# Flamingo-style layer pair: the second cross-attention's keys and queries stacked in half precision, scaled by the context's largest magnitude

## The reference, cut to what matters

```python
x = x + tanh(g_xattn[0]) * cross_attention_0(layernorm(x), ctx, mask)    # first stage
x = x + tanh(g_ffn[0])   * ffn_0(layernorm(x), w_up, w_down)             # ternary weights
x = x + tanh(g_xattn[1]) * cross_attention_1(layernorm(x), ctx)          # the stage of the change
x = x + tanh(g_ffn[1])   * ffn_1(layernorm(x), weight1, weight2, weight3)

def cross_attention_1(qkv, y):          # qkv (4, 512, 512), y (4, 1601, 512)
    bs, width, length = qkv.shape
    ch = width // 16                     # 16 heads of 32 channels
    q = qkv.reshape(bs * 16, ch, length)
    k = v = y.reshape(bs * 16, ch, -1)   # the context's memory read as (channels, 1601)
    scale = 1.0 / sqrt(sqrt(ch))
    weight = softmax(einsum('bct,bcs->bts', q * scale, k * scale))
    return einsum('bts,bcs->bct', weight, v).reshape(bs, -1, length)
```

## Time and profile before

| | |
|---|---|
| median of 3 runs | 1842.4 us (1840.54 to 1844.35) |
| the profiled execution: time, span | 1841.3 us, 1839.5 us |
| TensorE matmuls busy | 1658.9 us (90%), 7540 |
| TensorE weight loads busy | 800.2 us (44%), beside the matmuls |
| VectorE, ScalarE, GpSimd busy | 1147.0, 760.9, 843.0 us |
| mean granted clock of TensorE | 0.959 of 2.4 GHz |

### The profile page before, as it was taken

How to read it: one execution, slowest core, us unless ns; L and a number is a source line. 1 busy time by engine, 2 the same in 40 slices (tenths; PEclk the granted TensorE clock), 3 DMA queues, 4 the chain that set the end, 5 groups by cost and what they waited for, 6 DMA issues and landing times. The chain is left out here.

```text
span 1839.5 us, 22129 instructions
## 1 busy us (share of the span) xinstructions
PE 1658.9 (90%) x7540; PEld 800.2 (44%) x7568; DVE 1147.0 (62%) x1529; ACT 760.9 (41%) x1241; POOL 843.0 (46%) x340
## 2 busy tenths in 40 slices
PE   5999999898777876899999999899999997799898
PEld 2454444444433333444444444444444432344443
DVE  3669989884455557676766676667676630444543
ACT  1321211211543431566666666566666665111110
POOL 0022234544221125577778888677777877000000
PEclk9999999899899995999999999999999999799999
DMA  8232223322111115444333334444433310400000
GB/s 320 80 120 77 83 93 96 103 100 79 39 30 35 34 41 137 113 114 112 77 96 89 98 97 113 114 113 113 113 88 90 77 46 1 95 23 0 23 23 23
DMA packets 134316, 152.57 MB, mean 83 GB/s; under 512 B 59694, under 2 KB 101826, under 8 KB 134214
## 3 DMA queue, kind: packets, MB, share of 16 engines
q1 hardware_dynamic: 129222, 140.76, 29.3%
q10 hardware_dynamic: 4992, 10.49, 1.7%
HBM read 73.42 MB, written 10.76 MB: 46 GB/s over the span
## 5 line engine op out<-in xcount | busy, mean ns | idle before, releaser
L1352 DVE TENSOR_REDUCE c_piece_max<-c_unit 128x1 f32<-128x804 f32 x512 | 485.0, 984 | 241.0 <-PE c_unit L1490 238.4
L1448 ACT ACTIVATE c_prob<-c_scores 128x512 f32<-128x512 f32 (+1 forms) x832 | 473.3, 596 | 267.3 <-PE c_scores L1507 250.5
L1287 POOL TENSOR_TENSOR c_prob_sum<-c_prob_sum,c_prob 128x2048 f32<-128x2048 f32 x96 | 439.4, 4577 | 12.0 <-ACT c_prob L1448 6.0
L1507 PE MATMUL c_scores<-c_queries,c_keys 98*128 98x512 f32 (+1 forms) x832 | 354.8, 443 | 32.7 <-ACT c_prob L1448 17.4
L1490 PE MATMUL c_unit<-c_khigh,c_qdiag 128*128 128x402 f32 x1024 | 303.2, 381 | 20.1 <-DMA c_qdiag<-c_qhigh 10.1
L1490 PEld LDWEIGHTS c_unit<-c_khigh,c_qdiag 128*128 128x128 f32 x1024 | 186.6, 198 | 150.1 <-DVE c_piece_max L1352 90.1
L1507 PEld LDWEIGHTS c_scores<-c_queries,c_keys 98*128 98x128 f32 (+1 forms) x832 | 152.4, 186 | 202.0 <-ACT c_prob L1448 141.3
L1516 PE MATMUL c_out<-c_prob,c_VT 128*32 128x512 f32 (+1 forms) x1664 | 220.8, 610 | 0.0
L641 PE MATMUL a_S<-a_ctxT,a_xnT 128*128 128x401 f32 x512 | 190.7, 517 | 7.2 <-ACT a_prob L598 3.9
L671 PE MATMUL a_o<-a_ctx,a_probT 128*128 128x512 f32 (+1 forms) x416 | 181.2, 592 | 0.0
L1287 POOL TENSOR_TENSOR c_prob_sum<-c_prob 128x2048 f32<-128x2048 f32 x16 | 73.5, 4592 | 121.1 <-ACT c_prob L1448 121.1
(11 more groups left out here) (196 smaller groups left out, 1975.0 us busy)
## 6 DMA issues: line engine op xcount, KB each, us to landing
c_keys<-c_khigh SPq DMA_DIRECT2D x128, 200.2 KB, 3.0
c_k<-in_keys SPq DMA_DIRECT2D x16, 801.0 KB, 6.3
c_keys<-c_k SPq DMA_DIRECT2D x64, 200.2 KB, 3.0
a_ctx<-in_ctx SPq DMA_DIRECT2D x12, 1024.0 KB, 6.8
c_VT<-in_values SPq DMA_DIRECT2D x16, 768.0 KB
a_ctxT<-in_ctxT SPq DMA_DIRECT2D x12, 802.0 KB, 4.7
c_queries<-c_qhigh SPq DMA_DIRECT2D x128, 64.0 KB, 2.6
a_weights<-in_L_ffn_weight SPq DMA_DIRECT2D x3, 1408.0 KB, 14.7
```

The source lines that it names most:

```text
L1287: nc.gpsimd.tensor_tensor(psum4[:], a[:], prob[(j * MC + c) % RING][:], ALU.add).then_inc(sums_taken, 2 if i == 1 else 1)
L1352: nc.vector.tensor_reduce(piece_max[j % 2][:, k // 2, k % 2:k % 2 + 1], U[bank(unit)][:, :, 0:PIECE], axis=AX.XY, op=ALU.max).then_inc(uni ...
L1448: nc.scalar.activation(prob[(j * MC + c) % RING][0:w, h, :], STp[h % 2][0:w, :], ACT.Exp, scale=SCALE).then_inc(exp_done, 1)
L1507: nc.tensor.matmul(STp[h % 2][0:w, :], K[p][:, h, c * P:c * P + w].bitcast(F32R), Q[p][:, h, :].bitcast(F32R), start=True, stop=True).then ...
```

## The change

Half precision (float16) takes the place of float32r in the rounded parts, the rests, the stacks `K` and `Q`, and the block diagonal. Float16 has less range, so the keys are scaled by 2^13 over the largest magnitude of the whole context, and the exponential's scale takes the factor back. For that the first stage reduces each batch's transposed context on VectorE (`context_top`, in steps 2, 6, 10 and 14), joins the four, sends 128 numbers through memory and back to all partitions (SyncE, two DMAs, ahead of the stores of the weights), and makes two factors (`context_scales`). The keys' rest, with the scale in one operation, goes to VectorE, into a buffer of its own; it stands behind the maximum of unit 6 of group g+2. The negative maxima are one half-precision row (times 1/512 against 512 in the keys' row) rather than two: ScalarE's rounding of them and GpSimd's rest go, the row's matmul waits for VectorE's join alone. The waits are renamed to match.

```diff
+KEY_RANGE = 2.0 ** 13
+KEY_SCALE = float(D // 16) ** -0.5
...
             def load_transposed(b):
+                if b > 0:
+                    sp.wait_ge(ctx_topped, b)
...
+            sp.wait_ge(ctx_topped, B + 1)
+            sp.dma_start(flat_ctx_top.rearrange("(p o) -> p o", o=1), ctx_tops[:, B:B + 1]).then_inc(ctx_top_out, 16)
+            sp.wait_ge(ctx_top_out, 16)
+            sp.wait_ge(bit_scales_ready, 1)
+            sp.dma_start(wtops_all[:, 0:P // 4, :].rearrange("p r k -> p (r k)"), flat_ctx_top.rearrange("(o r) -> o r", o=1).broadcast_to([P, P])).then_inc(ctx_top_loaded, 16)
...
+            def context_top(b):
+                for n in range(4):
+                    dve.wait_ge(ctxT_loaded[n], 16 * (b + 1))
+                nc.vector.tensor_reduce(ctx_tops[:, b:b + 1], CT[:], axis=AX.XY, op=ALU.max, apply_absolute_value=True).then_inc(ctx_topped, 1)
+                if b == B - 1:
+                    dve.wait_ge(ctx_topped, B)
+                    nc.vector.tensor_reduce(ctx_tops[:, B:B + 1], ctx_tops[:, 0:B], axis=AX.X, op=ALU.max).then_inc(ctx_topped, 1)
+
+            def context_scales():
+                steps, scales = Steps(dve, ctx_scale_steps), shared["ctx_scales"]
+                dve.wait_ge(ctx_top_loaded, 16)
+                steps.link(nc.vector.tensor_reduce(scales[:, 2:3], wtops_all[:, 0:P // 4, :].rearrange("p r k -> p (r k)"), axis=AX.X, op=ALU.max))
+                steps.link(nc.vector.tensor_scalar(scales[:, 3:4], scales[:, 2:3], 1e-30, 1.0 / KEY_RANGE, ALU.max, ALU.mult))
+                steps.did(nc.vector.reciprocal(scales[:, 0:1], scales[:, 3:4]))
+                steps.did(nc.vector.tensor_scalar(scales[:, 1:2], scales[:, 3:4], KEY_SCALE, None, ALU.mult))
+                steps.settle()
...
+                if k % ST == 2:
+                    context_top(k // ST)
...
             add_out(K - 2)
+            context_scales()
...
-        KA = KM + 2
+        KA = KM + 1
+        ONES = 2.0 ** 9
...
-        krest = [k[:].bitcast(F32R) for k in kt]
-        khigh = [sb(f"c_khigh{j}", [P, MK], F32R) for j in range(2)]
+        krest = [sb(f"c_krest{j}", [P, MK], F16) for j in range(2)]
+        khigh = [sb(f"c_khigh{j}", [P, MK], F16) for j in range(2)]
...
-        K = [sb(f"c_keys{j}", [KA, H, MK]) for j in range(2)]
-        Q = [sb(f"c_queries{j}", [KA, H, D]) for j in range(2)]
+        K = [sb(f"c_keys{j}", [KA, H, MK], F16) for j in range(2)]
+        Q = [sb(f"c_queries{j}", [KA, H, D], F16) for j in range(2)]
...
-                    sp.wait_ge(rests_ready, 2 * n + 2)
+                    sp.wait_ge(qrest_ready, n + 1)
+                    sp.wait_ge(krest_ready, n + 1)
...
-            def rest_of_k(n, j):
-                pool.wait_ge(khigh_ready, n + 1)
-                nc.gpsimd.tensor_tensor(krest[j], kt[j][:], khigh[j][:], ALU.subtract).then_inc(rests_ready, 1)
-
-            def rest_of_maxima(n):
-                pool.wait_ge(nhigh_ready, n + 1)
-                high, rest = [nparts[:, :, :, a].rearrange("p t h -> p h t") for a in range(2)]
-                nc.gpsimd.tensor_tensor(rest, nmax[:], high, ALU.subtract).then_inc(nparts_ready, 1)
...
+            def rest_of_k(n, j):
+                dve.wait_ge(khigh_ready, n + 1)
+                wait(dve, stacked, (n - 1) * STACKS)
+                nc.vector.scalar_tensor_tensor(krest[j][:], kt[j][:], key_scale, khigh[j][:], ALU.mult, ALU.subtract).then_inc(krest_ready, 1)
...
-                nc.vector.tensor_copy(nrow[:], U[bank(unit)][0:2 * H, 0, :]).then_inc(unit_read, 1)
+                nc.vector.tensor_scalar(nrow[:], U[bank(unit)][0:H, 0, :], 1.0 / ONES, None, ALU.mult).then_inc(unit_read, 1)
...
             statistics(0)
             statistics(1)
+            rest_of_k(0, 0)
...
+                    if main and more and unit[2:] == (j + 2, 6):
+                        rest_of_k(g + 2, j % 2)
                 if not main:
+                    rest_of_k(1, 1)
                     statistics(2)
...
-                nc.scalar.copy(khigh[j][:], kt[j][:]).then_inc(khigh_ready, 1)
+                nc.scalar.activation(khigh[j][:], kt[j][:], ACT.Copy, scale=key_scale).then_inc(khigh_ready, 1)
...
-            def high_of_maxima(n):
-                act.wait_ge(nmax_ready, n + 1)
...
             def rows(unit):
                 n = unit[1]
-                pe.wait_ge(nparts_ready, n + 1)
+                pe.wait_ge(nmax_ready, n + 1)
```

More of the change, by code:

```diff
@@ L127, in cross_attention_0 @@
         wtops_all = sb("a_wtops_all", [P, P, 4])
+        ctx_tops = sb("a_ctx_tops", [P, B + 1])
         BIT_PIECES = 4
@@ L1044, in cross_attention_1 @@
     X, ident, gates = shared["X"], shared["ident"], shared["gates"]
+    key_scale, score_scale = shared["ctx_scales"][:, 0:1], shared["ctx_scales"][:, 1:2]
     with ExitStack() as stack:
@@ L1417, in split_queries @@
                 x = X[:, bass.ds(n, 1), :].rearrange("p o d -> p (o d)")
-                wait(act, rests_ready, 2 * n - 1)
+                wait(act, qrest_ready, n)
                 nc.scalar.activation(xn[:], x, ACT.Identity, bias=nshift[:], scale=rstd[:]).then_inc(xn_ready, 1)
@@ L1424, in split_queries @@
                 nc.scalar.copy(qhigh[j][:], xn[:]).then_inc(qhigh_ready, 1)
-            def high_of_maxima(n):
-                act.wait_ge(nmax_ready, n + 1)
-                wait(act, unit_full, FULL0 + rows_place(n - 1) + 1 if not isinstance(n, int) or n > 0 else 0)
-                nc.scalar.copy(nparts[:].bitcast(F32R)[:, :, :, 0].rearrange("p t h -> p h t"), nmax[:]).then_inc(nhigh_ready, 1)
             def take_out(g):
@@ L1465, in slot @@
                         split_keys(g + 2, j % 2)
-                    if c == (8 if not isinstance(g, int) or g > 0 else 10) and nxt:
-                        high_of_maxima(g + 1)
                 if nxt:
@@ L1489, in pair @@
                     at = STARTS[2 * half + e]
-                    last = nc.tensor.matmul(U[bank(unit)][:, e, 0:PIECE], QZ[o][:, h, t * P:(t + 1) * P].bitcast(F32R), khigh[o][:, at:at + PIECE], start=True, stop=True)
+                    last = nc.tensor.matmul(U[bank(unit)][:, e, 0:PIECE], QZ[o][:, h, t * P:(t + 1) * P], khigh[o][:, at:at + PIECE], start=True, stop=True)
                 last.then_inc(unit_full, 1)
@@ L1494, in rows @@
                 n = unit[1]
-                pe.wait_ge(nparts_ready, n + 1)
+                pe.wait_ge(nmax_ready, n + 1)
                 pe.wait_ge(unit_read, rows_place(n) + 1)
                 for t in range(TB):
-                    last = nc.tensor.transpose(U[bank(unit)][0:2 * H, 0, t * P:(t + 1) * P], nparts[:, t, :, :].rearrange("p h a -> p (h a)"), ident[:])
+                    last = nc.tensor.transpose(U[bank(unit)][0:H, 0, t * P:(t + 1) * P], nmax[:, t, :], ident[:])
                 last.then_inc(unit_full, 1)
@@ L1815, in program @@
         weight_tops, bit_scales = weight_stats[:, 0:2], weight_stats[:, 2:4]
+        ctx_scales = stack.enter_context(nc.sbuf_tensor("ctx_scales", [P, 4], F32))
         gates = stack.enter_context(nc.sbuf_tensor("gates", [P, 4], F32))
```

51 lines of the change are left out of this document (23 added, 28 removed).

## The result

The changed kernel takes 1874.6 us in the median of 4 runs (1872.4 to 1878.4), the kernel before 1841.9 beside it: ratio 1.018, 95% interval 1.016 to 1.020. The profiled execution took 1873.7 us with a span of 1871.9. The forecast's sum was 1874.4, slower with a chance of 0.59. The total is right; of its terms several are not, and they cancel.

A forecast was written before the change was run, and what follows sets the result against it. Bound: a chain of exponential, score and output product in second cross-attention, not TensorE's busy time. 1841.3 + 8.4 (first stage) - 5.8 (prologue) + 3 (group 0) + 34 (groups 1-13) - 6.5 (groups 14, 15) = 1874.4 us; range 1806 to 1888.

The forecast's parts named there:

- The half-precision matmuls: Second cross-attention: shorter bare and hidden weight loads save 0.26 us a chunk, 3.1 us a group, 50.4 to 47.3.
- The stall and its clock: Second cross-attention: VectorE's rest waits for GpSimd's addition; chain stops 3.5 us, slow clock adds 2.2, 5.7 a group.
- Other parts 0: Outside the main terms: the stack's DMAs and SyncE's added waits, put at 0; the exponential's scale operand goes unmentioned.
- Groups 1 to 13: Second cross-attention: each group 53.0 us with the stall, 2.6 more than before, +34 us together.
- Granted clock under 0.95 in the slices of this stage: Sign for the second cross-attention: TensorE's granted clock falls below 0.95, with an idle of 3 to 4 us a group.
- Group 0: Second cross-attention's first group: 16 more units, VectorE nearly full and also given the rest, +3 us (0 to 6).
- groups 14 and 15: Second cross-attention's last groups: no keys' rest to make, so no stall, -3.2 us each, -6.5 together.
- The prologue: Second cross-attention's prologue: single row of maxima -2.6 us, shorter loads in 32 units -3.2, together -5.8 (-9 to -2).
- The first stage: Four context reductions of 6.85 us on VectorE: the second and third delay step 12's chain, +8.4 us (5 to 12).
- their chain had some 8 us to spare: First stage's end: the fourth reduction delays the last weights by 6.85 us, held to be covered by this slack.
- Rival 1: Keys' rest meets no addition, or the addition does not hold it: it costs 1 us a group, 1809; chance 0.31.
- Rival 2: Rest is blocked, but the clock stays at 2.4 GHz: 50.8 us a group, 1845 in total; chance 0.11.

The follow-up runs named there:

- e5: Changed kernel with unscaled keys (nothing measured or scaled), a number as the exponential's scale, keys' rest back on GpSimd behind the last addition: 1787.4 us, ratio 0.970.
- e2: Changed kernel with the exponential's scale as a number of this data, the measured scale left out there: 1875.9 us, ratio 1.018.
- e6: Changed kernel with keys' rest behind unit 11, a number as the exponential's scale, no context reductions (finding of the scale left out): 1793.0 us, ratio 0.973.
- e9: Changed kernel with the keys' rest behind unit 11 in place of unit 6, nothing else altered: 1828.4 us, ratio 0.993.
- e3: Changed kernel without the four context reductions, their DMAs and waits, both scales set to this data's numbers: 1856.7 us, ratio 1.008.
- e7: Changed kernel with its context reductions at other places of VectorE's order, their DMAs behind the weights' stores, nothing left out: 1862.5 us, ratio 1.010.
- e10: Changed kernel with the keys' rest in two halves of 801 columns, behind units 6 and 11: 1855.0 us, ratio 1.008.

## Why the prediction was right

Its mechanism was the one that the runs show: the rest on VectorE meets GpSimd's addition of probabilities, is held until it ends, TensorE stops behind it once a group, and the clock falls. Term by term:

- **The half-precision matmuls**, forecast -3.1 us a group. e5 measures -2.5 (50.4 to 47.9). The longest score is 404 ns for 503, as forecast for a bare load; the term is too large by 0.6, and how the 2.5 divides is not shown.
- **The stall and its clock**, forecast 3.5 + 2.2 = 5.7 for a request 0.7 us late. In e2, which is the kernel that the forecast had in mind (an exponential of 595 ns), the request was 0.71 us late, TensorE idle 3.79 us, and the group 53.7 against e6's 48.1: 5.6 us (5.3 by the means of 13 groups). In the changed kernel itself the request came 1.6 us late, the idle time was 2.58, and the price 3.7.
- **The exponential** is the term that the forecast did not have. "Other parts 0" took in that its scale became one value per partition; that costs 88 ns in each, and 1.2 us a group (e9 against e6). It also moved the request by 0.9 us and so made the stall cheaper, which is why leaving it out (e2) changed nothing: -1.2 and +1.9. The forecast's group of 53.0 was right because its errors are of one size: 2.0 too much for the stall against 0.6 too much for the matmuls, 1.2 for the exponential and 0.2 for the moved rest. Most of this is linked, as the exponential made the stall cheaper; that it comes out even is luck. The Trainium skill (ScalarE: Activation LUTs, "What ACT_TABLE_LOAD costs") gives about 93 ns for each operand of one value per partition; these runs have 88.
- **The sum of a group**: 50.4 - 2.5 (e5) + 0.2 (rest on VectorE, e6) + 1.2 (exponential, e9) + 3.7 (lock and clock) = 53.0.
- **Groups 1 to 13**, forecast +34, measured +24.8 (50.9 to 52.8 in the mean). The forecast took 2.6 us for each of the 13. But before, group 8 took 55.9, 5.5 more than its neighbours; after, its extra is 1.8. And in three groups the stall cost no clock, which saves 1.9 each.
- **The clock.** "Granted clock under 0.95 in the slices of this stage" was wrong, it was 0.97. After the stall TensorE mostly ran at 1.2 GHz for a few us, but not always: in 10 of 13 groups. These are two windows around the end of a stall of 2.36 us, in the group of 51.1 us, and of one of 2.58, in a group of 53:

```profile
955.00:962.00 7.00, 6.14 (x45) 1.95 (x45) 4.98 (x6) 3.13 (x5) 6.16 (x4) 1.00 0.01 1
1060.00:1067.00 7.00, 6.59 (x33) 1.92 (x37) 4.01 (x6) 2.69 (x5) 5.79 (x3) 0.77 0.02 3
```

  The difference, 1.9 us, is what the clock costs where it falls (2.2 forecast); the idle time itself costs 51.1 - 49.3 = 1.8, less than its 2.4 to 2.6 us, since part of it was a wait before too.
- **Group 0**, forecast +3, and **groups 14 and 15**, forecast -3.2 each. From the first score to the first sum it takes 60.7 us against 61.7, so -1.0. Groups 14 and 15 gained 1.2 and 0.1 us; with a fast exponential (e2) 2.7 and 3.7. Here the missing term shows bare. The prediction also read 48.5 us for such a group out of a window of 97; between the sums' matmuls it was 47.8 before.
- **The prologue**, forecast -5.8. From TensorE's stop to the first score it was 52.9 us and is 47.2: -5.7. The sign "the first scores at 732" left out the forecast's own +8.4; with it the forecast would be 740.6, and they came at 748.2.
- **The first stage**, forecast +8.4, measured +15.9 up to TensorE's stop ahead of the prologue. Step 12 moved by 10.0 us (331.90 to 341.87), the forecast's chain. The step that failed is "their chain had some 8 us to spare" of the last weights. They were 16.3 us late (the sixth of the weights before them was 9.4 late already, by what had moved step 12, and the fourth reduction added 6.8), and the 8 us belonged to VectorE's own wait for TensorE; the chain that counts goes from the weights to GpSimd's clips, to the store in ScalarE's queue, to the copies behind it.

In all, the 15 groups behind the first sum gave +23.4 (forecast +27.5) and everything ahead of it +9.1 (forecast +5.6). The first stage's 7.5 us too few, and 5.1 too few for groups 14 and 15, stand against 9.2 too many for groups 1 to 13 and 4.0 for group 0. That the total is met within 1 us is luck; that the kernel is slower, and why, is not.

Rival 1 (the request comes before the addition, 1809) did not happen, but a few units later it does: in e9 the rest comes after the last addition, in e6 it meets only its last microsecond, and e6 lies 0.2 us a group above e5, less than the 1 us of that rival. Rival 2 (blocked, but the clock stays) is what 3 of 13 groups did.

## What to carry to other kernels

When work moves from GpSimd to VectorE and both read tensors in SBUF, ask what GpSimd runs at that moment: what VectorE loses is the time until it ends, on top of its own work, and a place of a few units earlier or later makes the difference (53.0 to 49.3 us a group by one number). Then ask who waits for the result: a place too late (unit 14) held SyncE's queue of 24 copies and, behind them, the next group's first operand. Two costs that meet in one stall hide each other, so take them away together as well as singly: the exponential's scale alone gave nothing (1874.6 to 1875.9), with the rest moved it gave 1.2 us a group. Reductions of 27 us cost 18 where they were put (e3) and some 4 to 6 at other places of the same queue (e7 against e3: 4.1 at the first sum, 5.8 by the totals).

## What the runs showed of the hardware

- VectorE's rest, with two inputs in SBUF, was held up by GpSimd's additions (4.57 us in place of 1.89). Its maxima of 128x804, with one input in PSUM, kept their 985 ns in the mean beside the same additions.
- The lock is mutual. A GpSimd operation on one value per partition, 192 ns alone, took 1.78 us behind a VectorE instruction of 1602 columns and 0.95 us behind one of 801.
- An exponential on 128x512 from PSUM takes 596 ns with a number as scale and 684 with one value per partition.
- A weight load of 97 or 98 rows by 128 columns takes 190 ns from the float32r tiles and 97 to 99 from half precision, while the shortest score of 512 columns, its load hidden, differs little: 389 against 377.
- An idle time of TensorE of 2.35 to 2.65 us was followed by a stretch at 1.2 GHz in 10 of 13 groups of the changed kernel; one of 3.5 to 3.8 us (e2) in 13 of 13; one of 1.5 to 2.0 us (e10) in 5 of 13.
